# When ScalarE takes the exponential of a local attention, and when VectorE adds its result to x: two orders changed in a software pipeline

## The chip, the core and the metric

The program runs on one core of one Trainium2 chip. The metric is the device time of one execution in microseconds. Shown are the median of three runs and, beside it, the one execution that the hardware profiler recorded.

## What is computed

The input x has 16 sequences of 256 tokens with 128 channels. A first attention layer (16 heads of width 8) is applied once. Then come six layers, each a local attention and a feed-forward part. Everything that this document is about lies in the local attention of these six layers:

```python
for i in range(6):
    x = attn_layer(shift_tokens(x), Wqkv[i], q_scale[i], k_scale[i], Wo[i]) + x
    x = ffn_layer(shift_tokens(x), ln_g[i], ln_b[i], W1[i], b1[i], W2[i], b2[i]) + x

def attn_layer(x, Wqkv, qs, ksc, Wo):          # 16 heads of 64
    q, k, v = split(x @ Wqkv)
    q = l2norm(q) * qs;  k = l2norm(k) * ksc
    q, k = rotary(q), rotary(k)                # with a scale in the tables
    out = local_attention(q, k, v)             # windows of 32, each sees itself and the one before
    return out @ Wo
```

The l2norm needs the sum of squares of each head of q and of k. The local attention is a softmax over 64 keys, with its maximum subtracted before the exponential.

## The kernel before

**Tiling.** x is kept in SBUF, transposed, as `xT` (128 channels on the partitions, 4096 tokens along the row). The six layers work on blocks of 128 tokens: 32 blocks in a layer, 192 in all, two to a sequence. `t` numbers the steps; step `t` starts block `t` and carries on with older ones. `b = t % 2` says whether the newest block is the first or the second half of its sequence, and so an "even" step is one with `b == 0`.

**The software pipeline.** Each engine runs one function for each step (`step_pe`, `step_act`, `step_dve`, `step_pool`, `step_sp`), and each function issues its instructions in an order that is written out by hand. `pl.has(n)` asks whether block `t - n` exists, `blocks(pl, name, n, k)` is the semaphore value that says that block `t - n` has passed this point. Every engine takes its instructions strictly in the order written, so a wait holds all that stands behind it on that engine. `steps` runs 12 steps straight, then a hardware loop of 5 turns with 32 steps each, then 32 more steps straight with the drain. Step numbers 32, 64, 96, 128 and 160 are the first of a layer; the step before each also prepares the weights of the next layer.

**One step on TensorE** (`step_pe`): project q of block t (6 matmuls of 512 columns, `q_done`); transpose P of block t-3 through `PC` (8 transposes from `Sx`, `pT_done`; these wait for `x_updated` of block t-4, since `PC` held that block's output projection); project k (`k_done`); transpose q of block t-1 (`qkT_done`); P times V of block t-3 (`av_done`, 64 small matmuls); transpose k of block t-1, once the q transposes have been copied out of `PC` (`qkT_kept`); project v (`v_done`); matmuls of the feed-forward part (w1 and gate in even steps; w2 and transposes in odd ones); scores of block t-1 (32 matmuls, `s_done`); output projection of block t-3 (8 matmuls, `y_done`). A float32 matmul of these last three kinds counts twice in the rows.

**One step on ScalarE** (`step_act`): exp of block t-2 (L832, in place in `Sx`, waits for `shifted`); square of q of block t (L837, waits for `q_done`); copy of the transposes of P, block t-3 (L840, waits for `pT_done`); square of k (L845, waits for `k_done`); in even steps a tiny `ss` (L850); two copies of the q transposes (L855); copy of the attention output `oT` (L860); copy of the k transposes (L865); copy of v (L872); the pieces of the feed-forward part; the start of the norm (L901, L903).

**One step on VectorE** (`step_dve`): maximum over the scores of block t-2 (L998, waits for `s_done`), subtraction of it into `Sx` (L1002, `shifted`), update of x with the attention output of block t-4 (L1006, waits for `y_done`, gives `x_updated`), rotation of q (L973 and L977, waits for the square of q), sums of q's squares (L981), rotation of k, the mask for the next scores (L994), sums of k's squares, row sums of the exponentials (L1029, waits for `exp_done`) and their reciprocals, and then the feed-forward pieces.

**GpSimd** adds the halves of the rotation (L1101), scales q and k by their norms (L1080) and weighs P (L1112, after the reciprocals). **SyncE** issues the transfers; in odd steps it moves x to `xf` after `x_updated`.

TensorE's matmuls are all issued by one helper (L211) and its transposes by another (L214), so in the rows they show by their tiles: `pair` is a PSUM tile (`PA0`, `PA1`, `PB`, `PC`), `pair<-wq_h,xs_h` is a projection, `pair<-small,Sx` a transpose of P, `pair<-small,qk` of q or k, `pair<-PT,VB` P times V, `pair<-kT,qT` scores, `pair<-oT,wo_sb` the output projection.

Of the kernel before, what the change touches and what calls it, by code (L numbers as in the profile page):

```python
# [8 lines left out]
ALU = mybir.AluOpType  # L9
ACT = mybir.ActivationFunctionType  # L10
# [3 lines left out]
P = 128  # L14
# [55 lines left out]
def build(nc, x_in, w_first, wqkv, wo, qkscale, fw1, fw2, vectors, c_rot, c_small, out):  # L70
    ctx = ExitStack()
    with ctx:
        def sb(name, shape, dt=F32):
            return ctx.enter_context(nc.sbuf_tensor(name, shape, dt))

        def sem(name):
            return ctx.enter_context(nc.semaphore(name))
# [3 lines left out]
        xT = sb("xT", [P, TOKENS])  # L81
# [34 lines left out]
        Sx = sb("Sx", [P, 2, PAIRS, 2, KEYS])  # L116
# [15 lines left out]
        PA0, PA1, PB, PC = (ctx.enter_context(nc.psum_tensor(f"pair{i}", [P, 1024], F32)) for i in range(4))  # L132
# [23 lines left out]
        S = {n: sem(n) for n in (*STEP, *PER_SEQ, *LOADS, *PARTS, *ONCE, *FIRST, "xf0", "xf1", "vb0", "vb1", "vb2", "vb3", "phase",   # L156
                                 "stored", "opened", "o_copied", "o_t", "o_sum", "zeroed",
                                 "cleared", "waited")}
# [35 lines left out]
        def bc(ap, n, inner):  # L194

            return ap.rearrange("p (n o) -> p n o", o=1).broadcast_to([P, n, inner])

        def rep(ap, n, inner):

            return ap.rearrange("p (o d) -> p o d", o=1).broadcast_to([P, n, inner])  # L200

        def h3(ap, d):
            return ap.rearrange("p (n d) -> p n d", d=d)

        V_ = nc.vector
        T_ = nc.tensor
        A_ = nc.scalar
# [387 lines left out]
        def blocks(pl, name, back, k):  # L595

            per = STEP[name]
            return pl.times(NBLOCKS * per) + ((pl.t - back) * per + k)
# [57 lines left out]
        def feed_banks(t):  # L656

            other = projections(t)[1]
            return other[:, 0:UNIT], other[:, UNIT:2 * UNIT], PC[:, UNIT:2 * UNIT]
# [165 lines left out]
        def step_act(e, pl):  # L825
            t, r, b, now = pl.t, pl.t % RING, pl.t % BLOCKS, pl.t % 2
            one, other = projections(t)
            bank0, bank1, bank2 = feed_banks(t)
            if pl.has(2):
                e.wait_ge(S["shifted"], blocks(pl, "shifted", 2, 1))  # L830
                rows = Sx[:, now, :, :, :].rearrange("p a w k -> p (a w k)")
                A_.activation(rows, rows, ACT.Exp).then_inc(S["exp_done"], 1)  # L832
            if pl.has(0):
                e.wait_ge(S["q_done"], blocks(pl, "q_done", 0, 1))
                if pl.has(1):
# [2 lines left out]
            if pl.has(3):  # L838
                e.wait_ge(S["pT_done"], blocks(pl, "pT_done", 3, 1))
                A_.activation(PT[:, :, :].rearrange("p a q -> p (a q)"), PC[:, :], ACT.Copy).then_inc(S["pT_kept"], 1)  # L840
            if pl.has(0):
                e.wait_ge(S["k_done"], blocks(pl, "k_done", 0, 1))
                if pl.has(1):
                    e.wait_ge(S["summed"], blocks(pl, "summed", 1, 2))
                A_.activation(sq[:, 1, :], other[:, :], ACT.Square).then_inc(S["squared"], 1)  # L845
# [5 lines left out]
            if pl.has(1):  # L851
                e.wait_ge(S["qkT_done"], blocks(pl, "qkT_done", 1, 1))
                for odd in range(2):
                    rows = slice(odd * DH, (odd + 1) * DH)
# [111 lines left out]
        def step_dve(e, pl):  # L966
            t, b, now = pl.t, pl.t % BLOCKS, pl.t % 2
# [16 lines left out]
            def write_mask(back):  # L984
# [8 lines left out]
                bb = (t - back) % BLOCKS  # L993
                V_.tensor_copy(h3(PB[:, :], P), rep(mask[:, bb * P:(bb + 1) * P], PAIRS, P)).then_inc(S["masked"], 1)  # L994

            if pl.has(2):
                e.wait_ge(S["s_done"], blocks(pl, "s_done", 2, 1))
                V_.tensor_reduce(mx[:, now, :], h3(PB[:, :], KEYS), axis=AX.X, op=ALU.max).then_inc(S["maxed"], 1)  # L998
                e.wait_ge(S["maxed"], blocks(pl, "maxed", 2, 1))
                if pl.has(4):  # L1000
                    e.wait_ge(S["pT_done"], blocks(pl, "pT_done", 4, 1))
                V_.tensor_tensor(Sx[:, now, :, :, :].rearrange("p a w k -> p (a w) k"), h3(PB[:, :], KEYS),  # L1002
                                 bc(mx[:, now, :], HEADS, KEYS), ALU.subtract).then_inc(S["shifted"], 1)
            if pl.has(4):
                e.wait_ge(S["y_done"], blocks(pl, "y_done", 4, 1))
                V_.tensor_tensor(xT[:, pl.columns(4)], PC[:, 0:P], xT[:, pl.columns(4)], ALU.add).then_inc(S["x_updated"], 1)  # L1006
            if pl.has(0):
                if t == 0:
                    e.wait_ge(S["tabled"], 1)
# [248 lines left out]
        @block.scalar  # L1258
        def _(act):
            act.wait_ge(S["zeroed"], 1)  # L1260
            A_.preload_act_table_set("natural_log_exp_and_others")
            first = Place(act, 0).at(0)
            act.wait_ge(S["w_loaded"], 16)
            act.wait_ge(S["v_cleared"], 1)
            first_stage(act, first_act)
            meet(act, 1)
            act.wait_ge(S["cleared"], 1)
            for q in range(2):
                round_x(act, first, q)
            steps(act, step_act)  # L1270
            meet(act, 2)
            finish(act, "act")

        @block.vector
        def _(dve):
            prepare(dve)
            first_stage(dve, first_dve)
            meet(dve, 1)
            clear(dve)
            steps(dve, step_dve)  # L1280
            meet(dve, 2)
            finish(dve, "dve")
# [54 lines left out]
```

## Time and profile before

| | us |
|---|---|
| median of 3 runs | 3418.71 (3418.09 to 3419.04) |
| the profiled execution | 3418.27 |
| its span in the profile | 3416.5 |
| TensorE busy | 3188.8 (93%) |
| VectorE busy | 2812.1 (82%) |
| GpSimd busy | 2626.1 (77%) |
| ScalarE busy | 2597.2 (76%) |
| granted TensorE clock, mean | 0.973 of full speed |

The span is the time from the first to the last instruction; the 1.8 us that the profiled execution has beyond it lie around the instructions. A busy TensorE is not TensorE at its peak: its matmuls overlap, and their ends are modelled. In the rows below a number in square brackets is the idle time of the engine just ahead of the instruction, with what ended it; times are in us from the start of the span. The steps at 1505 and 1536 us are odd, those at 1520 and 1552 us even.

### The profile page before, as it was taken

How to read it: one execution, taken by the hardware profiler on the slowest of the kernel's cores; microseconds unless marked ns; L12 is line 12 of the kernel's file. 1: busy time of each engine (PE TensorE's matmuls, PEld its weight loads, DVE VectorE, ACT ScalarE, POOL GpSimd, SP SyncE). 2: the span in 40 equal slices, each digit the busy share in tenths (PEclk: the TensorE clock that was granted, in tenths of full speed). 3: DMA queues.
4: the chain of work that ended last, by engine and by line, in shares of the span. 5: the costliest groups of instructions: out<-in, count | busy, mean ns of one | idle time of the engine just before them, and what ended most of it. 6: DMA issues, size and time to landing. Idle time of an engine off the chain costs nothing.

```text
span 3416.5 us, 133004 instructions
## 1 busy us (share of the span) xinstructions
PE 3188.8 (93%) x52802; PEld 2706.0 (79%) x52802; DVE 2812.1 (82%) x3743; ACT 2597.2 (76%) x3707; POOL 2626.1 (77%) x2593
## 2 busy tenths in 40 slices
PE   7978999989999989999989999989999999999996
PEld 4647888878788878888878888878888878888885
DVE  7967888888788888888888888888878888888882
ACT  6746778877787878778777877878778777878874
POOL 6648888878877878878878878877878887888871
PEclk9979999999999999999999999999999999999997
DMA  1001111111111111111101111111111111111111
GB/s 63 2 10 36 58 39 33 38 28 44 52 43 38 35 31 41 43 56 35 40 27 46 36 58 39 33 33 39 40 59 33 38 35 38 37 40 33 38 35 29
DMA packets 57827, 130.82 MB, mean 38 GB/s; under 512 B 10992, under 2 KB 33136, under 8 KB 56432
## 3 DMA queue, kind: packets, MB, share of 16 engines
q1 hardware_dynamic: 57200, 121.94, 12.2%
q8 instruction: 457, 7.49, 0.9%
q14 instruction: 170, 1.39, 0.1%
HBM read 19.17 MB, written 2.10 MB: 6 GB/s over the span
## 4 chain that ended last, share of the span: by engine, by line
PE 70%; ACT 15%; issue 8%; DVE 5%; POOL 2%; ACTq 0%; DMA 0%; POOLq 0%; DVEq 0%; SPq 0%
PE pair L211 56%; PE pair L214 13%; ACT qT L855 10%; ACT sq L845 3%; DVE ts L977 1%; ACT ss L850 1%; DVE ss L981 1%; DVE mx L998 1%; DVE qk L973 0%; DVE pair L994 0%; DVE tab L955 0%; POOL qk L1080 0%; DVE tab L956 0%; DVE Sx L1002 0%; ACT sq L837 0%
## 5 line engine op out<-in xcount | busy, mean ns | idle before, releaser
L1101 POOL TENSOR_TENSOR qk<-qk,ts 128x1024 f32<-128x1024 f32 x384 | 912.4, 2385 | 228.8 <-DVE ts L977 213.5
L973 DVE TENSOR_TENSOR qk<-pair,tab 128x1024 f32<-128x1024 f32 x384 | 468.2, 1219 | 365.6 <-ACT sq L837 362.8
L1080 POOL TENSOR_TENSOR qk<-qk,rn 128x1024 f32<-128x1024 f32 x384 | 733.1, 1930 | 28.6 <-issue 13.5
L211 PE MATMUL pair<-wq_h,xs_h 128*128 128x512 f32 x1154 | 512.3, 444 | 31.6 <-issue 14.8
L832 ACT ACTIVATE Sx<-Sx 128x1024 f32<-128x1024 f32 x192 | 203.4, 1060 | 395.4 <-DVE Sx L1002 395.4
L214 PE MATMUL pair<-small,qk 128*128 128x128 f32 x3104 | 420.5, 279 | 75.4 <-ACT qT L855 54.5
L1112 POOL TENSOR_TENSOR Sx<-Sx,rden 128x1024 f32<-128x1024 f32 x192 | 365.3, 1902 | 157.2 <-DVE rden L1032 157.2
L211 PE MATMUL pair<-wq_h,xs_l 128*128 128x512 f32 x1152 | 469.7, 408 | 0.4
L211 PE MATMUL pair<-wq_l,xs_h 128*128 128x512 f32 x1152 | 468.4, 407 | 0.0
L977 DVE TENSOR_TENSOR ts<-pair,tab 128x1024 f32<-128x1024 f32 x384 | 466.0, 1214 | 0.0
L981 DVE TENSOR_REDUCE ss<-sq 128x16 f32<-128x1024 f32 x384 | 463.9, 1208 | 0.0
L214 PEld LDWEIGHTS pair<-small,qk 128*128 128x128 f32 x3104 | 338.0, 143 | 154.7 <-issue 106.1
L211 PEld LDWEIGHTS pair<-kT,qT 128*64 128x64 f32 x12288 | 374.4, 138 | 36.2 <-issue 36.2
L211 PE MATMUL pair<-kT,qT 128*64 128x64 f32 x12288 | 400.6, 224 | 2.2 <-DVE pair L994 1.9
L855 ACT ACTIVATE qT<-pair 64x1024 f32<-64x1024 f32 x384 | 389.3, 1014 | 8.0 <-PE pair L214 5.1
L211 PE MATMUL pair<-oT,wo_sb 128*128 128x128 f32 x3072 | 394.5, 282 | 0.0
L211 PE MATMUL pair<-PT,VB 64*64 64x32 f32 x12288 | 375.6, 221 | 5.5 <-issue 3.1
L211 PE MATMUL pair<-PT,VA 64*64 64x32 f32 x12288 | 371.8, 220 | 0.6 <-issue 0.6
L211 PEld LDWEIGHTS pair<-oT,wo_sb 128*128 128x128 f32 x3072 | 358.3, 192 | 12.8
L211 PEld LDWEIGHTS pair<-PT,VB 64*64 64x64 f32 x12288 | 327.5, 135 | 36.5 <-issue 36.4
L211 PEld LDWEIGHTS pair<-PT,VA 64*64 64x64 f32 x12288 | 328.5, 135 | 2.1 <-issue 2.1
L214 PE MATMUL pair<-small,Sx 128*128 128x128 f32 x1792 | 246.5, 283 | 49.2 <-DVE xT L1006 39.7
(126 smaller groups left out, 6678.6 us busy)
## 6 DMA issues: line engine op xcount, KB each, us to landing
VB<-VA SPq DMA_DIRECT2D x192, 384.0 KB, 3.5
VB<-VA SPq DMA_DIRECT2D x96, 128.0 KB, 3.5
wq_raw<-wqkv SPq DMA_DIRECT2D x6, 1536.0 KB, 7.2
xf<-xT SPq DMA_DIRECT2D x96, 64.0 KB, 1.9
xf<-xT SPq DMA_DIRECT2D x96, 63.8 KB, 2.0
wo_sb<-wo SPq DMA_DIRECT2D x6, 512.0 KB, 3.6
X<-x_in SPq DMA_DIRECT2D x4, 512.0 KB, 7.6
out<-X SPq DMA_DIRECT2D x8, 256.0 KB, 2.3
```

What stands on the lines that cost most here:

```text
L211: return T_.matmul(out, lhsT, rhs, start=start, stop=stop, **k)
L214: return T_.transpose(out, in_, ident if idn is None else idn)
L832: A_.activation(rows, rows, ACT.Exp).then_inc(S["exp_done"], 1)
L845: A_.activation(sq[:, 1, :], other[:, :], ACT.Square).then_inc(S["squared"], 1)
L850: A_.activation(ss[:, 2 * HEADS:NORMS], f_mv[:, :, 1], ACT.Identity, bias=eps[:, 0:1]).then_inc(S["varied"], 1)
L855: last = A_.activation(qT[rows, :, :, odd * WIN:(odd + 1) * WIN], PC[rows, :].rearrange("p (a w q) -> p a w q", a=PAIRS, w=4), ACT.Copy)
L973: V_.tensor_tensor(h3(qk[:, now, kind, :], DH), h3(source[:, :], DH), rep(tab[:, 2 * kind, b, :], HEADS, DH), ALU.mult)
L977: V_.tensor_tensor(ts[:, kind, :].rearrange("p (h a c) -> p h a c", **halves), swapped, sines, ALU.mult).then_inc(S["rotated"], 1)
L981: V_.tensor_reduce(ss[:, kind * HEADS:(kind + 1) * HEADS], h3(sq[:, kind, :], DH), axis=AX.X, op=ALU.add).then_inc(S["summed"], 1)
L1080: G_.tensor_tensor(x, x, bc(rn[:, then, kind * HEADS:(kind + 1) * HEADS], HEADS, DH), ALU.mult).then_inc(S["scaled"], 1)
L1101: G_.tensor_tensor(qk[:, now, kind, :], qk[:, now, kind, :], ts[:, kind, :], ALU.add).then_inc(S["added"], 1)
L1112: G_.tensor_tensor(x, x, bc(rden[:, now, :], HEADS, KEYS), ALU.mult).then_inc(S["weighed"], 1)
```

## The change

ScalarE: the exponential moves from the head of the step to behind the square of q and the copy of the transposes of P, and so directly ahead of the square of k. VectorE: in even steps the update of x moves from behind the subtraction to between the maximum and the subtraction; in odd steps it stays where it was. No instruction is added or removed, and nothing changes on the other engines.

```diff
@@ step_act
-            if pl.has(2):
-                e.wait_ge(S["shifted"], blocks(pl, "shifted", 2, 1))
-                rows = Sx[:, now, :, :, :].rearrange("p a w k -> p (a w k)")
-                A_.activation(rows, rows, ACT.Exp).then_inc(S["exp_done"], 1)
             if pl.has(0):
                 e.wait_ge(S["q_done"], blocks(pl, "q_done", 0, 1))
...
             if pl.has(3):
                 e.wait_ge(S["pT_done"], blocks(pl, "pT_done", 3, 1))
                 A_.activation(PT[:, :, :].rearrange("p a q -> p (a q)"), PC[:, :], ACT.Copy).then_inc(S["pT_kept"], 1)
+            if pl.has(2):
+                e.wait_ge(S["shifted"], blocks(pl, "shifted", 2, 1))
+                rows = Sx[:, now, :, :, :].rearrange("p a w k -> p (a w k)")
+                A_.activation(rows, rows, ACT.Exp).then_inc(S["exp_done"], 1)
             if pl.has(0):
                 e.wait_ge(S["k_done"], blocks(pl, "k_done", 0, 1))
@@ step_dve
+            def update_x():
+                if pl.has(4):
+                    e.wait_ge(S["y_done"], blocks(pl, "y_done", 4, 1))
+                    V_.tensor_tensor(xT[:, pl.columns(4)], PC[:, 0:P], xT[:, pl.columns(4)], ALU.add).then_inc(S["x_updated"], 1)
+
             if pl.has(2):
                 e.wait_ge(S["s_done"], blocks(pl, "s_done", 2, 1))
                 V_.tensor_reduce(mx[:, now, :], ...).then_inc(S["maxed"], 1)
+            if b == 0:
+                update_x()
+            if pl.has(2):
                 e.wait_ge(S["maxed"], blocks(pl, "maxed", 2, 1))
...
                 V_.tensor_tensor(Sx[:, now, ...], ..., ALU.subtract).then_inc(S["shifted"], 1)
-            if pl.has(4):
-                e.wait_ge(S["y_done"], blocks(pl, "y_done", 4, 1))
-                V_.tensor_tensor(xT[:, pl.columns(4)], PC[:, 0:P], xT[:, pl.columns(4)], ALU.add).then_inc(S["x_updated"], 1)
+            if b == 1:
+                update_x()
```

## Rows read from the trace of the kernel before

**Rows 1.** The page, chain that ended last, shares of the span by line.
```profile
PE pair L211 56%; PE pair L214 13%; ACT qT L855 10%; ACT sq L845 3%; DVE ts L977 1%; ACT ss L850 1%; DVE ss L981 1%; DVE mx L998 1%; DVE qk L973 0%; DVE pair L994 0%; DVE tab L955 0%; POOL qk L1080 0%; DVE tab L956 0%; DVE Sx L1002 0%; ACT sq L837 0%
```
**Rows 2.** Waits, whole span: who waited for whom, us in total, times, longest.
```profile
ACT Sx L832 <- DVE Sx L1002: 395.4, 192, 9.9
DVE qk L973 <- ACT sq L837: 362.8, 192, 6.7
...
PE pair L214 <- ACT qT L855: 54.5, 189, 2.2
...
PE pair L214 <- DVE xT L1006: 39.7, 6, 8.0
```
**Rows 3.** The chain in order of time: start us, us, what.
```profile
1507.06 0.87 PE pair L214 x8
1507.93 1.43 PE pair L211 x6
...
1516.78 5.39 PE pair L211 x86
...
1522.23 1.09 PE pair L214 x8
1523.32 1.45 PE pair L211 x6
...
1529.23 8.92 PE pair L211 x110
...
1554.42 1.56 PE pair L211 x6
...
1560.43 9.10 PE pair L211 x110
```
**Rows 4.** Timeline of TensorE: start us, us, instruction group, idle before.
```profile
1512.57 1.07 PE L214 MATMUL pair<-small,qk 128*128 128x128 f32 x8 [0.23 <-ACT qT L855]
...
1518.72 2.05 PE L211 MATMUL pair<-oT,wo_sb 128*128 128x128 f32 x16
...
1528.16 1.06 PE L214 MATMUL pair<-small,qk 128*128 128x128 f32 x8 [0.24 <-ACT qT L855]
```
**Rows 5.** Timeline of ScalarE, odd step at 1505 and even step at 1520.
```profile
1507.20 1.00 ACT L837 ACTIVATE sq<-pair 128x1024 f32<-128x1024 f32 x1
...
1508.11 1.02 ACT L840 ACTIVATE PT<-pair 128x1024 f32<-128x1024 f32 x1
...
1509.46 1.02 ACT L845 ACTIVATE sq<-pair 128x1024 f32<-128x1024 f32 x1 [0.34 <-PE pair L211]
...
1510.38 2.04 ACT L855 ACTIVATE qT<-pair 64x1024 f32<-64x1024 f32 x2
...
1521.83 1.06 ACT L832 ACTIVATE Sx<-Sx 128x1024 f32<-128x1024 f32 x1 [2.19 <-DVE Sx L1002]
1522.80 1.01 ACT L837 ACTIVATE sq<-pair 128x1024 f32<-128x1024 f32 x1
1523.70 1.01 ACT L840 ACTIVATE PT<-pair 128x1024 f32<-128x1024 f32 x1
1524.87 1.03 ACT L845 ACTIVATE sq<-pair 128x1024 f32<-128x1024 f32 x1 [0.16 <-PE pair L211]
```
**Rows 6.** Timeline of VectorE, even step at 1520.
```profile
1519.33 1.21 DVE L998 TENSOR_REDUCE mx<-pair 128x16 f32<-128x1024 f32 x1
1520.57 1.22 DVE L1002 TENSOR_TENSOR Sx<-pair,mx 128x1024 f32<-128x1024 f32 x1
1521.71 0.28 DVE L1006 TENSOR_TENSOR xT<-pair,xT 128x128 f32<-128x128 f32 x1
```
**Rows 7.** Timeline of VectorE, first step of a layer (t = 64).
```profile
1259.93 1.21 DVE L998 TENSOR_REDUCE mx<-pair 128x16 f32<-128x1024 f32 x1
...
1262.32 0.28 DVE L1006 TENSOR_TENSOR xT<-pair,xT 128x128 f32<-128x128 f32 x1
```
**Rows 8.** Windows, an early step: us, busy (instructions) by engine, PEclk, DMA, GB/s.
```profile
343.00:358.00 15.00, 13.68 (x254) 11.58 (x253) 13.17 (x18) 10.64 (x16) 14.17 (x14) 1.00 0.16 46
```

## The prediction

> **What bounds the kernel now.** I began with the page's chain of work that ended last. It lies on TensorE's projections, scores and products (L211, 56% of the span) and transposes (L214, 13%), but 13% lies on two ScalarE lines: the copies of the q transposes (L855) and the square of k (L845) [rows 1]. So I read the whole-span waits. The largest are the ones that the change goes for: ScalarE idles 395 us ahead of the exponential until VectorE has subtracted, and VectorE idles 363 us ahead of the rotation until q is squared [rows 2]. Neither engine is the bound, so these totals price nothing. TensorE's own waits do: 189 times, once in nearly every step, it stands ahead of the k transposes until ScalarE's L855 is done, 54.5 us in all; and 6 times ahead of the P transposes until x is updated, 39.7 us, up to 8.0 at once [rows 2].
>
> The chain in order of time shows the same shape in each step. From q_done (1507.06) TensorE runs 8 transposes of P in 0.87 and the k projection in 1.43, and k_done falls at 1509.36 [rows 3]. From there ScalarE carries the chain: square of k at 1509.46, the two copies from 1510.38 to 1512.42 [rows 5]. Meanwhile TensorE has the q transposes and P times V to do, and is through 0.23 us before the k transposes may start at 1512.57; in the even step it is 0.24 [rows 4]. After these transposes TensorE runs to the next q_done without a wait: 8.92 us of matmuls in one piece in the even step [rows 3]. **So the length of a step is set by how long after q_done the square of k starts on ScalarE.** What I have to price is this one distance, in odd and in even steps.
>
> **ScalarE, odd steps.** Now the square of q starts at 1507.20, the copy of P's transposes 0.91 later, and the square of k at 1509.46, which is 2.40 after q_done. The engine was idle 0.34 there until k_done [rows 5]; k_done, 2.30 after q_done, set it. With the exponential gone from the head of the step, the square of q can start 0.1 after q_done (the distance that the square of k has to k_done), at +0.12 with a margin, where it was at +0.14: next to nothing is gained. The copy follows at +1.02 (the transposes end at +0.87, so it could not be before +0.97), and takes 0.92 to the next start, one such instruction less the overlap seen from 1507.20 to 1508.11. The exponential is an operand of the same size; from its start at 1521.83 to the next at 1522.80 are 0.97 [rows 5]. The square of k then starts at 1.02 + 0.92 + 0.97 = +2.91 instead of +2.40: **0.50 later**. It had 0.43 to hide 0.97 in, and that is all.
>
> **ScalarE and VectorE, even steps.** q_done is at 1516.78 + 5.39 = 1522.17 [rows 3]. Here the exponential, late since VectorE came to the maximum late, held the square of q until 1522.80 [rows 5], 0.5 more than q_done asks. The update of x, third on VectorE, ended at 1521.99 [rows 6], and TensorE started the P transposes 0.06 late and needed 1.09 where the odd step needs 0.87 [rows 3], so k_done came at +2.60. With x ahead of the subtraction, x waits for the output projection, which ends at 1518.72 + 2.05 = 1520.77 [rows 4]; x then runs from 1520.87 to 1521.15, and TensorE is not held: k_done at +2.32, 0.28 earlier. But this buys nothing, because k_done no longer sets the square of k. ScalarE gives, as in the odd step, +0.12 (square of q), +1.02 (copy), +1.94 (exponential), +2.91 (square of k). Before it was at 1524.87, +2.70; in every second even step, where the k projection took 1.56 instead of 1.45 [rows 3], it was at about +2.81. **So 0.21 and 0.10 later, 0.155 in the mean.**
>
> **What the moves put behind a wait.** The subtraction slips from 1520.57 to about 1521.07 and ends at 1522.29; the exponential needs it at 1524.1, so 1.8 us cover it. The rotation of q can start 0.5 earlier, and nothing that TensorE waits for hangs on it. The exponential ends at 1510.0 in the odd step instead of 1507.3; the row sums that read it come behind the rotations and masks, microseconds later on VectorE, and GpSimd's weighing of P behind those. If that cover were gone, each microsecond would delay the next P transposes by as much. SyncE's transfers of x hang on x_updated in odd steps alone, where VectorE's order stays. No instruction and no DMA is added, on any queue.
>
> **The first step of a layer** (5 of them, t = 32 to 160). VectorE comes late from preparing weights and tables; its maximum starts at 1259.93 and x is updated at 1262.32 [rows 7], and TensorE waits for that, up to 8.0 us [rows 2]. With x directly behind the maximum it starts at about 1261.06: 1.25 earlier. q has long been squared by then, the copy and the exponential fit ahead of k_done because TensorE takes longer there, and so all of it counts: 5 x 1.25 = **6.3 us gained**. Some three even steps at the start of the pipeline have the same shape, about 1 us each, an estimate from that row: 3 us.
>
> **The sum.** Odd steps 5 to 191: 94 x 0.50 = 47.0. Even steps 12 to 190 without those five: 85 x 0.155 = 13.2. Less 6.3 and 3. Together 50.9 slower. The profiled execution took 3418.27 us (3416.5 of span and 1.8 around it), 0.44 under the median of 3418.71, which is no difference here; 3418.3 + 50.9 gives **3469 us**.
>
> **Bounds.** The exponential behind a copy has no row. At the least it costs 0.90, the shortest step between two of these instructions [rows 5]: 0.07 less on 179 steps, 3457 in all. At the most it costs its full 1.06 and 0.1 for a wait that is not passed ahead of time: 0.19 more, 3503. I take 0.97, the row of the exponential itself. A second unknown is TensorE's supply of instructions: the same 110 matmuls take 8.92 in one even step and 9.10 in another [rows 3]. If the longer stand at the k transposes lets the queue fill, up to 0.18 on half of the even steps, some 9 us, comes back: 3448 with the low end above.
>
> **The price by the skill.** By row, an exponential costs 1.06 and a copy of the same size 1.02 [rows 5], so nearly alike. The Trainium skill, page "ScalarE: Activation LUTs", section "What ACT_TABLE_LOAD costs", says that an ACTIVATE with immediate operands takes 186 ns + 0.833 ns for each element and that neighbours overlap by about 93 ns, whatever the function. For 1024 elements that is 1.04 less 0.09, 0.95, and an estimate by it would be some 4 us under my sum. The row of this trace decides.
>
> **Rivals.**
> - *The k transposes are not really held by ScalarE.* The releaser is inferred. If it were TensorE's own work that paces the step, the exponential would be free, and k_done 0.28 earlier would count: 85 x 0.28 = 24, with 6.3 and 3 some 33 us faster, **3385**. It decides if P times V ends more than 0.5 us after the copies of L855; the rows have it 0.23 before the transposes start [rows 4]. Against it. Chance 0.08.
> - *Everything is hidden.* VectorE's head start or the fuller queue gives back what ScalarE loses, and the time stays at **3418**. For it speaks only that the granted sizes are small (0.50 of a step of 15.5). Chance 0.04.
> - *The clock falls.* An early step with TensorE busy 13.68 of 15.00, 91%, still has the granted clock 1.00 [rows 8], the 2.4 GHz level, and after the change TensorE is busier than that. If it fell all the same to the 1.2 GHz level for one k projection in each odd step, that would double 1.43 us [rows 3]: 94 x 1.43 = 134 on top of my sum, **3603**. Chance 0.03. The Trainium skill, page "TensorE: Matmul & The Clock Gate", section "A second HAM failure mode: psum-queue depth-cycling", says that frequent micro-idles between groups of matmuls can make the clock oscillate. Here every step has had such a gap, and no row shows it.
>
> **Numbers.** My own case has 0.85: 3469. The range 3446 to 3494 takes in the low end with the queue's gift and most of the high one. A measurement of this kernel can tell 0.2%, 7 us, from no change. Slower by more: 0.85 + 0.03; within: 0.04; faster: 0.08.
>
> **What would show it.** Right: ScalarE's idle ahead of the exponential is nearly gone (it was 395); the wait of the k transposes for L855 rises from 54 to some 130 us (0.23 + 0.5 in odd, 0.24 + 0.44 in even steps, since k_done comes earlier there); the square of k starts 2.91 after q_done in both kinds of step; the wait for x at layer starts shrinks by 6. Wrong: the exponential takes less than 0.9 between copy and square; the even steps' q_done to square of k stays under 2.7; the piece of matmuls from the k transposes to q_done changes its length; or the clock's mean leaves 0.97.

## The result and the profile after

The changed kernel took 3474.9 us (median of 4 runs, 3469.7 to 3476.9) against 3418.9 before (now of four as well), a ratio of 1.0159 (95% interval 1.0142 to 1.0177): 54 us slower by the ratio, 56 by the medians. The profiled execution took 3476.8 (span 3475.0), 58.6 more than the profiled one of before. The forecast was 3469, range 3446 to 3494.

The page's chain that ended last, shares by line (compare [rows 1]):

```profile
PE pair L211 51%; ACT qT L855 10%; PE pair L214 9%; ACT sq L845 5%; ACT PT L836 5%; ACT sq L833 5%; ACT Sx L840 2%; ACT ss L850 0%; DVE wq_l L963 0%; DVE tab L955 0%; POOL sq L399 0%; DVE VB L321 0%; POOL wq_l L963 0%; DVE qk L317 0%; DVE mx L1003 0%
```

Three ScalarE lines have joined the chain: the square of q (L833), the copy of P's transposes (L836) and the exponential (L840). TensorE's two lines lost 9 points. The waits of the whole span (us in total, times, longest; compare [rows 2]):

```profile
ACT sq L833 <- PE pair L211: 494.5, 191, 8.2
...
DVE qk L973 <- ACT sq L833: 286.2, 187, 6.7
...
PE pair L214 <- ACT qT L855: 140.1, 189, 2.2
...
PE pair L214 <- DVE xT L999: 24.5, 6, 4.9
```

ScalarE's idle of 395 us ahead of the exponential has not been used: it moved ahead of the square of q and grew to 494. VectorE's wait for that square fell by 77 us, which TensorE never sees. What it does see is the third line: 54.5 before, 140.1 now, and that is the loss. The timeline of ScalarE, an even step and an odd one (compare [rows 5]; q_done is at 1538.80 and 1555.18):

```profile
1538.90 1.02 ACT L833 ACTIVATE sq<-pair 128x1024 f32<-128x1024 f32 x1 [2.66 <-PE pair L211]
1539.87 1.03 ACT L836 ACTIVATE PT<-pair 128x1024 f32<-128x1024 f32 x1
1540.92 1.06 ACT L840 ACTIVATE Sx<-Sx 128x1024 f32<-128x1024 f32 x1
1541.88 1.01 ACT L845 ACTIVATE sq<-pair 128x1024 f32<-128x1024 f32 x1
...
1555.29 1.02 ACT L833 ACTIVATE sq<-pair 128x1024 f32<-128x1024 f32 x1 [2.12 <-PE pair L211]
1556.21 1.02 ACT L836 ACTIVATE PT<-pair 128x1024 f32<-128x1024 f32 x1
1557.11 1.06 ACT L840 ACTIVATE Sx<-Sx 128x1024 f32<-128x1024 f32 x1
1558.06 1.02 ACT L845 ACTIVATE sq<-pair 128x1024 f32<-128x1024 f32 x1
```

Four instructions stand without a gap from q_done to the square of k, which starts 2.88 after q_done in the odd step and 3.08 in the even one. From there on next to nothing has changed (from the start of the k transposes to the next q_done 10.21 in even steps, before 10.24, and 9.61 in odd ones in both kernels, means); the even step's run of matmuls from the k transposes to the next q_done is as long as it was (8.92 and 9.10 in [rows 3]), here in the chain in order of time, where the first piece ends at q_done:

```profile
1535.92 2.88 PE pair L211 x19
...
1546.22 8.96 PE pair L211 x110
```

I read these distances off the timelines for all steps of the hardware loop but the first of a layer and of a turn. Times are in us after q_done, medians; "T end" is the end of the transposes of P. The last column alone is a mean, of the start of the k transposes, which is what sets the step.

| kernel, steps | T end | k_done | square of k | k transposes (mean) |
|---|---|---|---|---|
| before, even | 1.15 | 2.66 | 2.78 | 6.05 |
| before, odd | 0.88 | 2.29 | 2.40 | 5.51 |
| after, even | 1.07 | 2.59 | 3.12 | 6.38 |
| after, odd | 0.87 | 2.29 | 2.89 | 5.99 |

The odd steps lost 0.48 and the even ones 0.33. By the last block's square of k 58.9 us were lost: 67.8 on the 169 steps from 13 on that start neither a layer nor a turn of the loop, 3.2 on the six at the turns and ends of the loop, less 6.6 on the first steps of the layers, and less 5.4 up to step 11 (1.2 of it in the first stage, which the change doesn't touch). At the start of a layer the chain shows VectorE's new order (t = 64; compare [rows 7]): x is updated 1.13 after the maximum begins, where it was 2.39.

```profile
1273.79 1.13 DVE mx L1003
1274.92 0.21 DVE xT L999
```

### The profile page after: what moved, and what is told of

It is laid out like the page before. It is cut to its first block, busy times and chain, and to the rows that moved or that the text cites. A ratio compares the mean times of both kernels' runs of the same rounds, so it can differ in the third digit from the quotient of the medians.

```text
span 3475.0 us, 133009 instructions
## 1 busy us (share of the span) xinstructions
PE 3180.8 (92%) x52802; PEld 2709.4 (78%) x52802; DVE 2827.8 (81%) x3743; ACT 2585.6 (74%) x3707; POOL 2625.7 (76%) x2593
## 4 chain that ended last, share of the span: by engine, by line
PE 60%; ACT 29%; issue 7%; DVE 2%; POOL 1%; ACTq 0%; DMA 0%; DVEq 0%; POOLq 0%; SPq 0%
PE pair L211 51%; ACT qT L855 10%; PE pair L214 9%; ACT sq L845 5%; ACT PT L836 5%; ACT sq L833 5%; ACT Sx L840 2%; ACT ss L850 0%; DVE wq_l L963 0%; DVE tab L955 0%; POOL sq L399 0%; DVE VB L321 0%; POOL wq_l L963 0%; DVE qk L317 0%; DVE mx L1003 0%
## 5 line engine op out<-in xcount | busy, mean ns | idle before, releaser
L833 ACT ACTIVATE sq<-pair 128x1024 f32<-128x1024 f32 x192 | 196.9, 1025 | 494.5 <-PE pair L211 494.5
L214 PE MATMUL pair<-small,qk 128*128 128x128 f32 x3104 | 421.2, 279 | 156.5 <-ACT qT L855 140.1
L211 PE MATMUL pair<-wq_h,xs_h 128*128 128x512 f32 x1154 | 513.0, 445 | 40.0 <-issue 14.9
L855 ACT ACTIVATE qT<-pair 64x1024 f32<-64x1024 f32 x384 | 389.0, 1013 | 6.7 <-PE pair L214 4.3
L211 PEld LDWEIGHTS pair<-wq_h,xs_h 128*128 128x128 f32 x1154 | 222.6, 193 | 74.9 <-issue 26.9
```

Source lines behind the costliest of these rows:

```text
L211: return T_.matmul(out, lhsT, rhs, start=start, stop=stop, **k)
L214: return T_.transpose(out, in_, ident if idn is None else idn)
L833: A_.activation(sq[:, 0, :], one[:, :], ACT.Square).then_inc(S["squared"], 1)
L855: last = A_.activation(qT[rows, :, :, odd * WIN:(odd + 1) * WIN], PC[rows, :].rearrange("p (a w q) -> p a w q", a=PAIRS, w=4), ACT.Copy)
```

## The experiments

Theory A: a step is as long as ScalarE's queue from q_done to the square of k makes it, or k_done where that is later. The times of one kernel vary by some tenths of a per cent between runs, so a ratio is given with its interval, against the kernel before in the same session on the same chip, and the distances carry the verdicts.

**e1: only ScalarE's order changed.** L840 to L843 as in the change, `step_dve` as before.

> The exponential moved as in the change, VectorE's order left as before. Theory A (the step is as long as ScalarE's queue from q_done to the square of k makes it): odd steps as in the changed kernel, square of k 2.88 after q_done; even steps wait for the late x (transposes of P end 1.15 after q_done), square of k at 3.05 to 3.2; no gain at the 5 layer starts. Time 3484 to 3495, 10 to 20 over the changed kernel. Rival B (the move of x is what costs in the changed kernel): under 3475, near 3460. A detail to read: the changed kernel's even steps show 1.05 from the copy to the exponential where odd steps show 0.90. If the later subtraction causes it, it is 0.90 in even steps here; if not, 1.05.

3476.6 us, ratio 1.0196 (1.0170 to 1.0222): 60 us lost by the medians, 67 by the ratio. The time is under the 3484 that I had expected at the least. ScalarE's timeline, even step, q_done at 1542.92:

```profile
1543.03 1.03 ACT L833 ACTIVATE sq<-pair 128x1024 f32<-128x1024 f32 x1 [2.65 <-PE pair L211]
1544.01 1.03 ACT L836 ACTIVATE PT<-pair 128x1024 f32<-128x1024 f32 x1
1545.06 1.06 ACT L840 ACTIVATE Sx<-Sx 128x1024 f32<-128x1024 f32 x1
1546.03 1.01 ACT L845 ACTIVATE sq<-pair 128x1024 f32<-128x1024 f32 x1
```

This is the changed kernel's step: 6.38 to the k transposes in even steps, 6.00 in odd. The whole loss belongs to the exponential's move, and rival B falls by these distances; the time alone, 3476.6 where the rival has less than 3475, would not decide it. I had expected steady even steps to be slower here than in the changed kernel, since x stays late; they aren't. T ends at 1.07 in both, so x is no longer what holds the transposes. The steps have grown, VectorE's work has not, and so its x now arrives earlier as TensorE sees it: it is updated 0.56 ahead of q_done, where it was 0.18 ahead in the kernel before (medians of even steps). The first steps of the layers are where the two kernels differ: 139.0 us for the five here, 133.3 in the changed kernel, 139.9 before (square of k to square of k). And the exponential starts 1.05 after the copy here too, so the later subtraction isn't the reason.

**e2: only VectorE's order changed.** `update_x()` as in the change, `step_act` as before.

> The update of x moved as in the change, ScalarE's order left as before. Theory A: in even steps the subtraction ends 0.5 later, the exponential at the head of ScalarE's step waits for it, and square of q, copy and square of k come 0.2 later: 85 x 0.2 = 17 lost; 6.5 gained at the 5 layer starts and some 3 at the start: 3418 + 17 - 9.5 = 3426 (3418 to 3432). Rival C (the k transposes are paced by TensorE, x early is a pure gain): 3385 to 3400.

3452.2 us, ratio 1.0125 (1.0099 to 1.0150): the direction was right (rival C falls), but 36 us by the medians and 43 by the ratio were lost where I had expected 8, and 3432 at the most. ScalarE's timeline in an even step, q_done at about 1530.99:

```profile
1531.08 1.06 ACT L832 ACTIVATE Sx<-Sx 128x1024 f32<-128x1024 f32 x1 [2.62 <-DVE Sx L1010]
1532.05 1.01 ACT L837 ACTIVATE sq<-pair 128x1024 f32<-128x1024 f32 x1
1532.95 1.02 ACT L840 ACTIVATE PT<-pair 128x1024 f32<-128x1024 f32 x1
1533.85 1.03 ACT L845 ACTIVATE sq<-pair 128x1024 f32<-128x1024 f32 x1
```

TensorE's timeline in the same step, its q transposes:

```profile
1534.11 1.06 PE L214 MATMUL pair<-small,qk 128*128 128x128 f32 x8 [0.62 <-ACT PT L840]
```

The square of k is 0.1 later in the mean, less than expected, but the k transposes are 0.36 later (6.41 after q_done). The second fence says why. The q transposes write `PC` and must wait until ScalarE has copied P's transposes out of it. TensorE stands 0.62 for that copy, L855 then waits for the q transposes, and everything behind is late. **There is a second chain**: exponential, square of q, copy of P's transposes, q transposes, L855. Before the change it only just touched: the copy started at 1.53 and ended at 2.55, k_done was at 2.66, and the q transposes stood 0.06 for the copy in the mean of the even steps (0.52 here). My expectation left it out.

**e3 and e4: the exponential where TensorE does not feel it.** e3 puts it behind the copy of the k transposes; e4 adds the early x.

```diff
@@ step_act, exponential taken from the changed place
             if pl.has(1):
                 e.wait_ge(S["qkT_done"], blocks(pl, "qkT_done", 1, 2))
                 bb = (t - 1) % BLOCKS
                 A_.activation(kT[:, :, WIN + bb * P:WIN + (bb + 1) * P], h3(PC[:, :], P), ACT.Copy).then_inc(S["qkT_kept"], 1)
+            if pl.has(2):
+                e.wait_ge(S["shifted"], blocks(pl, "shifted", 2, 1))
+                rows = Sx[:, now, :, :, :].rearrange("p a w k -> p (a w k)")
+                A_.activation(rows, rows, ACT.Exp).then_inc(S["exp_done"], 1)
```

> The exponential behind the copy of the k transposes, ahead of the copy of v; VectorE's order as before. Nothing but the square of q and the copy of P's transposes stands between q_done and the square of k. Theory A: the square of k starts 0.1 after k_done in both kinds of step, at 2.40 and 2.70 to 2.81 after q_done as before, so 3418 within 5. Rival D (the place of the exponential as such costs, wherever it interrupts the copies that TensorE waits for): near 3475.

> As the run before, and the update of x ahead of the subtraction in even steps. Theory A: now k_done sets the square of k, and k_done earlier by 0.13 in even steps (2.47 after q_done in the changed kernel's trace, 2.60 before) counts: 85 x 0.13 = 11, with 6.5 at layer starts and 3 at the start: 3398 (3392 to 3404). If x early is worth nothing in steady steps: 3409. Rival D: near 3470.

e3: 3426.0 us, ratio 1.0042 (1.0020 to 1.0064). e4: 3414.3 us, ratio 0.9994 (0.9981 to 1.0007). Rival D falls: the same exponential, elsewhere in the queue, costs a quarter of it or nothing. Both came out over my number: e3 by 8 us in the median and 14 by the ratio, e4 by 16 and 18, so that e4 is not told from the kernel before, where I had expected it 20 us faster. e4, even step, q_done about 1510.11:

```profile
1512.71 1.03 ACT L841 ACTIVATE sq<-pair 128x1024 f32<-128x1024 f32 x1 [0.49 <-PE pair L211]
1513.76 0.30 ACT L846 ACTIVATE ss<-f_mv,eps 128x2 f32<-128x2 f32 x1
```

The square of k starts as forecast, 0.1 after k_done. But the next instruction follows at 1.05 where [rows 5] and the changed kernel have 0.90 to 0.92. It does so in e3 too, and so e3's k transposes are 0.09 late in even steps; in odd ones 0.06, because there k_done itself is 0.05 late: 85 x 0.09 + 94 x 0.06 = 13 us, e3's loss (14 by the ratio, 10 by the medians). For e4, k_done came only 0.07 earlier than before in even steps, not 0.13 (2.57 against 2.64 in the mean, both counted over all steps; my 2.47 was one step). Against e3, e4 won 5.9 at the layer starts (133.1 against 139.0).

**e5: half of the exponential in the changed place,** half in e3's, x early.

```diff
-                A_.activation(rows, rows, ACT.Exp).then_inc(S["exp_done"], 1)
+                A_.activation(rows[:, 0:512], rows[:, 0:512], ACT.Exp)
@@ behind the copy of the k transposes
+                A_.activation(rows[:, 512:1024], rows[:, 512:1024], ACT.Exp).then_inc(S["exp_done"], 1)
```

> The changed kernel with the exponential cut in two: columns 0 to 511 at the changed place, columns 512 to 1023 where the late kernel (e4) has the whole of it. Theory A says that work ahead of the square of k is free up to k_done and costs in full beyond it. Half an exponential adds about 0.53 to the queue: the square of k then starts 2.48 after q_done in odd steps (0.05 later than in e4) and 2.70 in even ones (as in e4): within 5 us of e4, 3414 to 3424. Rival E (cost in proportion to the work placed there): halfway from e4 to the changed kernel, near 3444.

3409.8 us, ratio 0.9970 (0.9958 to 0.9982). Even step, q_done about 1511.11:

```profile
1513.24 0.63 ACT L840 ACTIVATE Sx<-Sx 128x512 f32<-128x512 f32 x1
1513.78 1.01 ACT L845 ACTIVATE sq<-pair 128x1024 f32<-128x1024 f32 x1
```

Half an exponential costs 0.54 of queue, as expected, and the square of k starts at 2.71 in even and 2.46 in odd steps, only 0.04 and 0.08 later than 0.1 after k_done. With the whole of it there the kernel takes 65 us more (1.0159 against 0.9970). The cost is a threshold and not a proportion; rival E falls. The kernel is a little faster than before, by 6.6 at the layer starts and by the early steps. By the ratios it is also 8 us faster than e4, where I had expected no more than 5 of difference: the start at 1.05 falls between copy and exponential here, ahead of k_done and hidden by it, and not behind the square of k, so the k transposes start 0.11 earlier in even steps (6.00 against 6.11).

**e6, e7, e8: why the even steps' transposes end late.** `FILL` gives the number of filler instructions (semaphore increments) that TensorE has between and behind the matmuls of the projections: 39 to 48 in even steps, 20 to 22 in odd ones. These three cut the even ones to 21: e6 in the kernel before, e7 in e4, e8 in the changed kernel.

```diff
-        FILL = (43, 21, 46, 21, 44, 22, ...)
+        FILL = (21, 21, 21, 21, 21, 22, ...)
```

> The kernel before, with TensorE's filler instructions (semaphore increments between matmuls of the projections) cut from 39 to 48 a step to 21 in even steps, as odd steps have. Question: are the fillers why the transposes of P end 1.07 after q_done in even steps and 0.87 in odd ones, whatever VectorE does? If so: 0.9 to 0.95 in even steps here, k_done at 2.35. Theory A with its second chain (exponential, square of q, copy of P's transposes, and only then the q transposes, which overwrite PC) says that this is worth little here, since the copy ends at 2.55 after q_done as before: within 6 us of the kernel before. If k_done alone set the step: 20 us faster. If the fillers are of use elsewhere it could be slower.

> e4 (exponential behind the copy of the k transposes, x early) with the same cut of the fillers. Nothing of ScalarE stands ahead of k_done any more, so k_done 0.25 to 0.3 earlier in even steps counts in full: 80 steps, 20 to 28 us under e4, near 3390, and faster than both kernels.

> The changed kernel with the same cut. Here ScalarE's queue ends after k_done, so k_done 0.25 earlier buys nothing; what can be gained is that the copy of P's transposes no longer waits (1.10 to 1.04) and perhaps the 0.15 that the exponential takes more behind it in even steps than in odd ones: square of k at 2.90 to 3.05 instead of 3.12, 6 to 18 us under the changed kernel. If it reads 0.90 from copy to exponential in even steps, the late transposes were the reason of the 1.05.

| kernel | us | ratio (95%) | T end, even | k_done | square of k | k transposes (mean) |
|---|---|---|---|---|---|---|
| e6 | 3417.7 | 0.9996 (0.9985 to 1.0007) | 1.15 | 2.55 | 2.66 | 6.12 |
| e7 | 3393.4 | 0.9918 (0.9899 to 0.9938) | 0.87 | 2.28 | 2.39 | 5.88 |
| e8 | 3466.9 | 1.0144 (1.0122 to 1.0166) | 0.87 | 2.28 | 3.05 | 6.32 |

These three separate the causes best. The same cut moves k_done by 0.3 in e7 and in e8. In e7, where k_done sets the step, the square of k starts 0.30 earlier than in e4 in the mean of the even steps and the k transposes 0.24; in e8, where ScalarE's queue ends 0.8 after k_done, both move by 0.06 to 0.07. By the times e7 won 21 us over e4 by the medians (26 by the ratios), e8 5 (1.0144 against 1.0159, intervals that overlap) to 8 over the changed kernel.

The whole times hold three more things that the cut does and that the expectations price at nothing. The even steps' matmuls from the k transposes to the next q_done take 0.1 less (10.04 against 10.14 in e7, 10.03 against 10.14 in e8, medians). TensorE's four stands at the jump of the hardware loop went from 15.7 to 8.0 us in all in e7 (against e4) and from 14.9 to 8.6 in e8. Against that TensorE now stands in the middle of P times V, with nothing in the profile to wait for, in e7 in about every fifth step: 37 stands of over 0.4 us with 33 us in all in e7, 32 with 28 us in e8, 33 with 28 us in e6; e4, the changed kernel and the kernel before have 3, 3 and 4 of them, with 3 to 5 us. So the k transposes of e7's odd steps start at 5.58 in the median as in e4 (5.57), but at 5.80 in the mean. That e7 came out at the forecast 20 to 28 us under e4 is in part luck: the gains and the loss here nearly cancel.

In e6 T still ends at 1.15: there the late x holds the transposes. k_done comes 0.11 earlier all the same, but the q transposes now stand 0.17 for the copy of P's transposes, the second chain, and the k transposes start only 0.09 earlier in the median (5.98 against 6.07); the stands in P times V make their mean later than before. So there were two floors under "T end" in the kernel before, 1.15 from x and 1.07 from the fillers, and taking away only the upper one, as the change does, could give 0.08 and not 0.28. e8 also tells that the late transposes are not why the exponential takes 1.05:

```profile
1532.53 1.02 ACT L836 ACTIVATE PT<-pair 128x1024 f32<-128x1024 f32 x1
1533.58 1.06 ACT L840 ACTIVATE Sx<-Sx 128x1024 f32<-128x1024 f32 x1
1534.54 1.00 ACT L845 ACTIVATE sq<-pair 128x1024 f32<-128x1024 f32 x1
```

The copy does not wait here (0.92 after the square of q), and the exponential still follows at 1.05.

**e9 and e10: how far it goes.** e9 is e5 with the cut, e10 is e7 with no fillers at all.

> The halved exponential (e5) with TensorE's fillers cut to 21 in even steps. Theory A: in even steps ScalarE's queue with half an exponential ends at 2.6 to 2.7 after q_done and k_done at 2.28, so the queue is now the longer of the two, and the cut buys less than it did for e7: 0 to 8 us under e5, 3402 to 3410. If k_done set the step in e5's even steps alone and the queue were shorter: 20 us under e5, near 3390.

> e7 (late exponential, x early) with no fillers at all in any step. If fillers delay k_done in odd steps too, it moves from 2.36 towards 2.2 after q_done and the time falls some 10 us under e7, to 3380. If 21 fillers already pass beside the matmuls (k_done 2.28 with them in even steps): the same as e7 within 5, 3386 to 3398.

e9: 3384.5 us, ratio 0.9914 (0.9891 to 0.9937), 0.9% faster than the kernel before, with e7 the best of the study. In the steady even steps the square of k starts at 2.62 as expected, and the k transposes came 0.08 earlier in the mean than e5's, 6 to 7 us. I expected 0 to 8 in all, and 19 were won (0.9970 against 0.9914). About 10 are at the turns of the hardware loop, and some 18 in the even steps' matmuls from the k transposes to the next q_done (10.03 against 10.25 in the median); stands in P times V, as in e7, took 12 back in odd steps (all by the profiled executions, which are 23 us apart). TensorE's timeline at the head of a turn in e5:

```profile
924.31 0.79 PE L211 MATMUL pair<-wq_h,xs_h 128*128 128x512 f32 x1 [3.96 <-issue]
```

The same place in e9:

```profile
921.41 0.50 PE L211 MATMUL pair<-wq_h,xs_h 128*128 128x512 f32 x1 [1.88 <-issue]
```

The stand at the jump is 1.88 instead of 3.96, and the matmul behind it takes 0.50 instead of 0.79. Fewer instructions alone do not shorten it, though: e10, with none of the fillers, has the long stand again:

```profile
924.26 0.79 PE L211 MATMUL pair<-wq_h,xs_h 128*128 128x512 f32 x1 [4.08 <-issue]
```

e10: 3409.2 us, ratio 0.9988 (0.9973 to 1.0002), slower than e7 by 0.7%. k_done is where it was (2.28 and 2.37), so the 21 do pass beside the matmuls, but TensorE's waits with nothing to wait for grew from 42.3 to 53.7 us, and the mean time from the square of k of an even step to that of the odd one behind it from 15.99 to 16.19. I had not expected that. What grew are the four jumps (14.6 us in all, against 8.0) and the stands in P times V (39 with 40 us, against 37 with 33), such as this one:

```profile
603.88 0.24 PE L211 MATMUL pair<-PT,VB 64*64 64x32 f32 x2 [1.29 <-issue]
```

So the fillers have a use: with those of the kernel before, these stands are all but absent. What makes them come is not tested.

## Why the prediction was right, and where its parts were not

- **The bound.** "The length of a step is set by how long after q_done the square of k starts on ScalarE": shown, by e1 (the loss without the move of x), e3 and e4 (no loss of that size with the exponential elsewhere), e5 (the threshold) and the pair e7 and e8 (k_done matters in one and not in the other). It was incomplete: e2 showed the second chain over the copy of P's transposes, which the change itself does not touch, since it starts that copy earlier.
- **Odd steps,** 0.50 forecast, 0.48 measured. The 2.91 was 2.89; the exponential behind a copy costs 0.90 and ahead of a square 0.95, so neither bound was needed.
- **Even steps,** 0.155 forecast, 0.33 measured; this is the term that was mis-sized, by 85 x 0.175 = 15 us. Two parts: T ends at 1.07 and not at 0.87, which puts the copy at 1.10 instead of 1.02, and the exponential follows the copy at 1.05 instead of 0.92. The first comes from the fillers (e8). The second stays open: not the subtraction (e1), not the late transposes (e8). That the total is off by only 3 to 8 us (54 to 59 measured, 51 forecast) is in part luck: the early steps, the odd steps and the layer starts together gave back some 7 of the 15 us, and the medians and the ratio have 56 and 54 us where the profiled execution lost 59.
- **"k_done at +2.32, 0.28 earlier" with x early:** wrong. I read the late x as the reason of the whole difference between even and odd steps; it was 0.07 to 0.08 of 0.36 (2.64 and 2.28, means). The cut of the fillers took off the other 0.3: 0.2 ahead of the end of the transposes, 0.1 in the k projection. That is also the reason of the 1.56 instead of 1.45 of [rows 3], which are steps with 46 and with 45 fillers; with 47 and 48 it is 1.72. The error cost nothing since k_done did not count, as the step itself said.
- **Layer starts,** 6.3 forecast, 6.6 measured. The early steps gave 4.2 back (5.4 with the first stage), where my sum had 3 for the even ones among them and charged 2 for the odd ones. The gift of a fuller queue, up to 9 us, was 2 (10.24 to 10.21 in even steps).
- **The wait for L855,** "some 130 us": 140.1. The wait for x at layer starts was to shrink by 6; it went from 39.7 to 24.5. Only 6 of the 15 are the early x (34.1 in e4); the others come with the exponential's move, by which TensorE comes later to that wait (30.6 in e1, with x late).
- **The exponential's idle, "nearly gone":** right, and worth nothing, as the waits of an engine off the chain are.
- **The rivals.** TensorE as the pacer (3385): its signature would have been e2 faster than before; it was 1.25% slower. That everything is hidden (3418): the result rules it out. The clock: the granted clock is 1.00 in both kinds of step with 0.7 to 0.8 us of standing still in each, and 0.975 over the span (0.973 before).

```profile
1538.80:1555.18 16.38, 15.54 (x270) 13.84 (x271) 13.39 (x16) 13.47 (x17) 11.39 (x12) 1.00 0.09 26
1555.18:1570.77 15.59, 14.88 (x261) 12.67 (x259) 13.55 (x19) 11.55 (x17) 14.04 (x13) 1.00 0.16 45
```

These are windows over one even and one odd step (us, busy time and instructions by engine, then PEclk): TensorE is busy 95%. Two such steps do not show that the clock can't fall for that reason, only that it did not here. The Trainium skill (page "TensorE: Matmul & The Clock Gate", section "A second HAM failure mode: psum-queue depth-cycling") says that frequent micro-idles between groups of matmuls can make the clock oscillate; the windows above, with 1.00 in both steps, do not show it. The Trainium skill's figures for an ACTIVATE (page "ScalarE: Activation LUTs", section "What ACT_TABLE_LOAD costs") give an estimate of 0.95 from start to start for 1024 elements; that fits odd steps (0.90 and 0.95) and not the 1.05 of even ones.

## What to carry to other kernels

A long idle ahead of an instruction is not a place to save: see what the next consumer on the bounding engine waits for, and count the queue from the last event that this engine gives to the one that it needs back. Work put into that stretch is free up to the slack (0.43 us in the odd steps here) and costs in full beyond it; half an exponential nearly fitted (0.06 late), a whole one cost 1.6%. And look for other chains that end at the same wait, as e2 shows. When one cause of a delay is to be taken away, look for the floor that the next cause has put just under it.

## What the runs showed of the hardware that was not expected

- Two ScalarE instructions in a row start 0.90 to 0.97 apart when they overlap, and 1.05 in even steps behind the copy (e1, e5, e8, e9, the changed kernel) or behind the square of k (e3, e4, e7, e10). The durations are the same. What takes the overlap away is open.
- Semaphore increments between TensorE's matmuls are free up to a point. With 20 to 22 in a step nothing is lost against none (k_done at 2.28 in the even steps of e7 and of e10). With 44 to 48 the q projection still takes 1.65 in the changed kernel, but k_done is 0.2 to 0.4 later, and where the delay lands differs by step: with 44 or 45 the transposes of P end at 1.06 to 1.15 and the k projection takes 1.65 to 1.68; with 46, 1.08 and 1.79; with 48, 0.87 (as with 21) and 1.96 (medians of the changed kernel's even steps, first start to last end).
- Too few of them cost as well: with 20 to 22 or none in all steps, TensorE stood 31 to 39 times for over 0.4 us inside P times V, 26 to 40 us in all (e6 to e10), and 2 to 5 times, 1 to 5 us, in all other kernels but e2 (9 times, 10 us). The reason is open.
- At the jump of a hardware loop TensorE stood 3.2 to 4.2 us with the fillers of the kernel before and with none (e10), and 1.9 to 2.4 us with 20 to 22 in each step (e6 to e9). The granted clock behind the first jump was 0.50 over 2.7 us in e5 (1.2 GHz) after a stand of 3.96, and 1.00 over 2.6 us in e9 (2.4 GHz) after one of 1.88; in between, it was 0.81 in e7 after 2.12. e5 and e9:

```profile
924.30:927.00 2.70, 2.69 (x6) 1.79 (x7) 1.20 (x2) 0.00 (x0) 2.70 (x2) 0.50 0.78 225
921.40:924.00 2.60, 2.59 (x15) 1.95 (x15) 2.55 (x3) 0.58 (x1) 1.77 (x1) 1.00 0.44 95
```
